# Combined convolution weights from 32-row groups in four row places, with a new order of the first steps

## The reference

```
p = hidden_states @ in_proj_w.T
h, gate = (p[..., :256], p[..., 256:])
conv = conv_general_dilated(h, conv_w, padding=[(3, 0)], feature_group_count=8) + conv_b
h = conv * silu(gate)
residual = h
hn = layernorm(h, ln_g, ln_b)
h = silu(hn @ fc_w.T + fc_b) @ cproj_w.T + cproj_b + residual
return h @ out_w.T
```

## Time and profile before

| | us |
|---|---|
| median of three runs | 369.46 (369.4 to 369.9) |
| the profiled execution's own time | 370.72 |
| its span, first to last instruction | 368.9 |
| TensorE busy | 323.3 (88%) |
| Vector busy | 261.1 (71%) |
| Scalar busy | 210.0 (57%) |
| GpSimd busy | 173.4 (47%) |

### The profile page before, as it was taken

The page is one execution under the profiler, slowest core; times in us unless marked ns, Lnnn a source line. Parts: engine busy times, 40 slices in busy tenths (PEclk is TensorE's granted clock), DMA queues, the critical chain, the costliest instruction groups (busy, mean ns, idle before and its releaser), DMA issues.

```text
span 368.9 us, 8839 instructions
## 1 busy us (share of the span) xinstructions
PE 323.3 (88%) x2692; PEld 295.2 (80%) x2692; DVE 261.1 (71%) x865; ACT 210.0 (57%) x430; POOL 173.4 (47%) x237
## 2 busy tenths in 40 slices
PE   3799999976777999999985989999798999999990
PEld 1789989866676999898975778888587999999990
DVE  3558988865873567769774699987796777677841
ACT  2354777635522355455438679898366668667330
POOL 1004677763464345886478677754211342244200
PEclk9999999987985999999999899999999999999997
DMA  8990011021132533421500300000000000000001
GB/s 274 431 367 1 16 37 40 29 61 29 43 97 59 186 85 92 140 60 53 165 23 29 115 2 2 3 3 0 3 3 0 2 16 16 14 14 0 16 14 32
DMA packets 17034, 23.73 MB, mean 64 GB/s; under 512 B 3424, under 2 KB 14176, under 8 KB 16208
## 3 DMA queue, kind: packets, MB, share of 16 engines
q1 hardware_dynamic: 13712, 17.97, 15.0%
q0 software_dynamic: 2272, 4.69, 3.9%
q10 hardware_dynamic: 1008, 0.53, 0.5%
HBM read 17.45 MB, written 6.73 MB: 66 GB/s over the span
## 4 chain that ended last, share of the span: by engine, by line
PE 44%; issue 12%; DVE 11%; POOL 9%; ACT 3%; POOLq 0%; DVEq 0%; ACTq 0%
PE ps L1985 8%; PE ps L1986 8%; PE ps L1817 6%; PE ps L1617 5%; POOL sb_w_lo L587 4%; PE ps L1619 4%; PE ps L1618 4%; PE ps L1806 3%; PE ps L2048 3%; POOL sb_xT_lo L580 1%; DVE sb_stage L1321 1%; DVE sb_x_in L1507 1%; POOL sb_rstd_hs L454 1%; PE ps L1782 1%; POOL answers L566 1%
## 5 line engine op out<-in xcount | busy, mean ns | idle before, releaser
L1985 PE MATMUL ps<-sb_w_hi,sb_fh_hi 128*128 128x256 f32 x256 | 61.2, 283 | 1.4 <-DVE sb_w_lo L925 0.7
L1986 PE MATMUL ps<-sb_w_lo,sb_fh_hi 128*128 128x256 f32 x256 | 59.8, 278 | 0.0
L1985 PEld LDWEIGHTS ps<-sb_w_hi,sb_fh_hi 128*128 128x128 f32 x256 | 48.2, 188 | 2.5 <-issue 1.1
L1986 PEld LDWEIGHTS ps<-sb_w_lo,sb_fh_hi 128*128 128x128 f32 x256 | 48.2, 188 | 0.0
L467 POOL DMA_INDIRECT routed<-sb_rows_of,sb_row x32 | 32.1, 1003 | 16.3 <-issue 10.1
L1617 PE MATMUL ps<-sb_w_hi,sb_rT_hi 128*128 x78 | 30.4, 390 | 7.3 <-issue 5.2
L1817 PE MATMUL ps<-sb_w,sb_stage 128*128 x234 | 34.9, 288 | 0.8 <-ACT sb_stage L752 0.8
L615 POOL TENSOR_TENSOR sb_w_lo<-sb_x_in,sb_w_hi 128x256 fp32r<-128x256 f32 x24 | 17.5, 757 | 35.4 <-DVE sb_w_hi L1553 35.4
L1817 PEld LDWEIGHTS ps<-sb_w,sb_stage 128*128 128x128 f32 x234 | 31.1, 202 | 1.2 <-issue 1.0
L566 POOL DMA_INDIRECT answers<-sb_stage x24 | 24.8, 1035 | 12.8 <-issue 8.2
L587 POOL TENSOR_TENSOR sb_w_lo<-sb_x_in,sb_w_hi 128x512 fp32r<-128x512 f32 x16 | 20.7, 1295 | 16.7 <-DVE sb_w_hi L1407 16.5
(11 more groups left out here) (308 smaller groups left out, 1031.0 us busy)
## 6 DMA issues: line engine op xcount, KB each, us to landing
sb_stage<-in_w SPq DMA_DIRECT2D x2, 1408.0 KB, 13.0
sb_stage<-routed SPq DMA_DIRECT2D x24, 65.0 KB
sb_w<-in_w SPq DMA_DIRECT2D x1, 1536.0 KB, 17.5
sb_x_in<-in_x_tok SPq DMA_DIRECT2D x1, 1024.0 KB, 8.7
sb_x_in<-in_ff_h SPq DMA_DIRECT2D x1, 1024.0 KB
sb_xT_in<-in_ff_h SPq DMA_DIRECT2D x1, 1024.0 KB
sb_got_first<-answers SPq DMA_DIRECT2D x4, 256.0 KB, 3.2
sb_w<-answers SPq DMA_DIRECT2D x4, 256.0 KB, 4.5
```

Source lines behind the costliest of these rows:

```text
L1985: mm(dst, w_hi, x_hi, start=start, stop=False)
L1986: last = mm(dst, w_hi, x_lo, start=False, stop=stop and exact)
```

## The change

`conv_own` holds, for each half, only the 32 by 32 blocks: 128 rows, two halves, 4 taps by 32 outputs, 128 KB. For each half TensorE makes four products of 32 rows and 128 columns; the group's rows select its place among the array's rows, and each of the eight products has a PSUM bank of its own. `front_of(t)` reads the four banks of a half in the order taps, groups, outputs. The first steps of the engines are put in another order:

```diff
@@ helpers
+        conv_own = conv_bd[:, :, 0:TAPS * GROUP_WIDTH]
+        def front_of(t):
+            return ps[:, t * GROUP_HEADS:(t + 1) * GROUP_HEADS, 0:TAPS * GROUP_WIDTH].rearrange("p g (k o) -> p k g o", o=GROUP_WIDTH)
@@ sync
-            for tile, src in ((w_h, "w_h"), (conv_bd, "conv_bd")):
+            for tile, src in ((w_h, "w_h"), (conv_own, "conv_own")):
                 sp.dma_start(tile[:, :, :], A[src]).then_inc(ld["front"], 16)
             sp.dma_start(xT_in[:, 0, :], A["xT"][:, 0, :]).then_inc(ld["x_first"], 16)
+            sp.dma_start(const[:, :], A["const"]).then_inc(ld["const"], 16)
+            sp.dma_start(conv_b[:, :], A["conv_b"]).then_inc(ld["bias"], 16)
@@ scalar
-            act.dma_start(const[:, :], A["const"]).then_inc(ld["const"], 16)
-            act.dma_start(conv_b[:, :], A["conv_b"]).then_inc(ld["bias"], 16)
-            for tile, src in ((ln_gb, "ln_gb"), (fc_b, "fc_b"),
-                              (cproj_b, "cproj_b"), (gate_wT, "gate_wT")):
+            for tile, src in ((ln_gb, "ln_gb"), (fc_b, "fc_b")):
                 act.dma_start(tile[:, :], A[src]).then_inc(ld["conv"], 16)
+            act.wait_ge(wt["memset"], MEMSETS)
+            nc.scalar.activation(touched[:, :], ones[:, 0:1], ACT.Silu)
...
-            for t in range(2):
+            def front_high(t):
                 act.wait_ge(wt["conv_mm"], t + 1)
-                nc.scalar.activation(front_hi[:, 0:TAPS, t * P:(t + 1) * P],
-                                     ps[:, t, :].rearrange("p (k o) -> p k o", o=P), ACT.Copy).then_inc(wt["front_hi"], 1)
+                nc.scalar.activation(front_hi[:, 0:TAPS, t * P:(t + 1) * P].rearrange("p k (g o) -> p k g o", o=GROUP_WIDTH),
+                                     front_of(t), ACT.Copy).then_inc(wt["front_hi"], 1)
...
             high_part(0)
+            for t in range(2):
+                front_high(t)
+            for tile, src in ((cproj_b, "cproj_b"), (gate_wT, "gate_wT")):
+                act.dma_start(tile[:, :], A[src]).then_inc(ld["conv"], 16)
             high_part(1)
-            act.wait_ge(wt["memset"], MEMSETS)
-            nc.scalar.activation(touched[:, :], ones[:, 0:1], ACT.Silu)
@@ tensor
             for t in range(2):
-                mm(ps[:, t, :], w_h[:, t, :], conv_bd[:, t, :], start=True, stop=True).then_inc(wt["conv_mm"], 1)
+                for g in range(P // GROUP_WIDTH):
+                    own = slice(g * GROUP_WIDTH, (g + 1) * GROUP_WIDTH)
+                    last = mm(ps[:, t * GROUP_HEADS + g, 0:TAPS * GROUP_WIDTH], w_h[own, t, :], conv_own[own, t, :], start=True, stop=True)
+                last.then_inc(wt["conv_mm"], 1)
...
-                    pe.wait_ge(wt["before"], 3)
+                    pe.wait_ge(wt["before"], 9)
```

More of the change, by code:

```diff
@@ L11 @@
 PAD = TAPS - 1
+GROUP_WIDTH = INNER // GROUPS
 EXPERTS, TOP_K, HIDDEN = 8, 2, 352
@@ L960, in _ @@
             V.memset(earlier[:, :, :], 0.0).then_inc(wt["before"], 1)
[L961 to L964, removed]
             V.memset(taken[:, :], 0.0).then_inc(wt["before"], 1)
@@ L969, in _, with low_part @@
             V.memset(upto_2[:, :], 0.0).then_inc(wt["before"], 1)
-            dve.wait_ge(wt["before"], 7)
+            dve.wait_ge(wt["before"], 6)
             V.memset(region_2[:, EXPERTS - 1:EXPERTS], -float((EXPERTS - 1) * REGION)).then_inc(wt["before"], 1)
+            def low_part(b):
+                dve.wait_ge(g0["x_hi"], b + 1)
+                wait(dve, g0["front"], b - 1)
+                V.tensor_tensor(xT_lo[:, b % 2, :], xT_in[:, b, :], xT_hi[:, b % 2, :].bitcast(fp32), ALU.subtract).then_inc(g0["x_lo"], 1)
+            dve.wait_ge(wt["front_hi"], 1)
+            V.tensor_tensor(front_lo[:, TAPS, :], w_gate[:, :], front_hi[:, TAPS, :].bitcast(fp32), ALU.subtract).then_inc(wt["front_lo"], 1)
+            low_part(0)
+            for t in range(2):
+                dve.wait_ge(wt["front_hi"], t + 2)
+                V.tensor_tensor(front_lo[:, 0:TAPS, t * P:(t + 1) * P].rearrange("p k (g o) -> p k g o", o=GROUP_WIDTH), front_of(t),
+                                front_hi[:, 0:TAPS, t * P:(t + 1) * P].bitcast(fp32).rearrange("p k (g o) -> p k g o", o=GROUP_WIDTH),
+                                ALU.subtract).then_inc(wt["front_lo"], 1)
+            dve.wait_ge(ld["const"], 16)
+            V.tensor_copy(before[:, :], const[:, C_BEFORE:C_BEFORE + P]).then_inc(wt["before"], 1)
+            V.tensor_scalar(base_row[:, :, :], const[:, C_BASE:C_BASE + EXPERTS].unsqueeze(1).to_broadcast([P, TILES, EXPERTS]),
+                            ident[:, 0:1], None, ALU.mult).then_inc(wt["before"], 1)
             V.tensor_copy(first_rows[:, :], const[:, C_ROW:C_ROW + max(PHASE_TILES)]).then_inc(wt["before"], 1)
@@ L998, in _ @@
             split3(conv_b3[:, :], whole_b, whole_b, b_part, b_rest, wt["conv_b3"])
-            dve.wait_ge(wt["front_hi"], 1)
-            V.tensor_tensor(front_lo[:, TAPS, :], w_gate[:, :], front_hi[:, TAPS, :].bitcast(fp32), ALU.subtract).then_inc(wt["front_lo"], 1)
-            for t in range(2):
-                dve.wait_ge(wt["front_hi"], t + 2)
-                V.tensor_tensor(front_lo[:, 0:TAPS, t * P:(t + 1) * P], ps[:, t, :].rearrange("p (k o) -> p k o", o=P),
-                                front_hi[:, 0:TAPS, t * P:(t + 1) * P].bitcast(fp32), ALU.subtract).then_inc(wt["front_lo"], 1)
             def small_weights():
@@ L1219, in _ @@
             h_flat = h[:, :, :].rearrange("p t f -> p (t f)")
-            def low_part(b):
-                dve.wait_ge(g0["x_hi"], b + 1)
-                wait(dve, g0["front"], b - 1)
-                V.tensor_tensor(xT_lo[:, b % 2, :], xT_in[:, b, :], xT_hi[:, b % 2, :].bitcast(fp32), ALU.subtract).then_inc(g0["x_lo"], 1)
-            low_part(0)
             dve.wait_ge(ld["conv"], 16 * 7)
@@ L2158, in layouts @@
     width = INNER // GROUPS
-    bd = np.zeros((2, P, TAPS, P), f)
-    for o in range(INNER):
-        t, g = o // P, o % P // width
-        bd[t, g * width:(g + 1) * width, :, o % P] = a["L0_attn_conv_w"][o]
-    A["conv_bd"] = np.ascontiguousarray(bd.reshape(2, P, TAPS * P).transpose(1, 0, 2))
+    by_group = a["L0_attn_conv_w"].reshape(2, P // width, width, width, TAPS)
+    A["conv_own"] = np.ascontiguousarray(by_group.transpose(1, 3, 0, 4, 2).reshape(P, 2, TAPS * width))
     A["conv_b"] = rows(a["L0_attn_conv_b"])
```

## The result

| | before | after |
|---|---|---|
| median, runs on one chip in turn | 369.43 (368.07 to 369.9, 4 runs) | 376.35 (375.35 to 378.4, 4 runs) |
| the profiled execution's own time | 370.72 | 376.35 |
| its span | 368.9 | 374.5 |

What follows compares the result with a forecast made beforehand. TensorE's back-to-back convolution batches were taken as the bound, handing on batch 0's shift. −0.3 us from `small_weights`' start and +0.9 from the clock made +0.6: span 368.9 to 369.5, median 370.1 us, range 368.2 to 372.3.

Steps and rivals of the forecast that it cites:

- The row places overlap: Combined weights on TensorE: 16 records overlap as column places do, taking 1.3 us and ending at 5.3.
- rival 1: Combined weights: row places don't overlap, products end at 7.8, loads land at 15.6 or later; 372.7 us; chance 15%.
- The gap on TensorE between front and `small_weights`: TensorE idles from 8.8 to 13.0 us, a gap of 3 to 5 us ended by `gate_wT`.
- rival 4: Small loads: their packets don't queue, so they land at 8.8 us; 365.4 us in all; chance 7%.
- the term of the two moved loads: `cproj_b` and `gate_wT`, issued later, land at 13.0 us; `small_weights` starts at 13.0 instead of 13.3, −0.3 us.
- The cross-check: Landing of `gate_wT`: its old 7.2 us copied onto an issue at 5.9 gives 13.1 us.
- The landing bounds of the range: Landing of the small loads: 11.0 us at the fast end (chance 20%), 15.6 or later at the slow end (15%).
- the clock: TensorE after the gap: rate rises 3.9 us after restart, at 16.9 against 16.27; the clock gives back 0.9 us.
- rival 2: TensorE after the gap: rate rises 5.5 us after restart, 370.9 us in all; later still, 371.5; chance 15%.
- the rest of `xT` to `w2` come about 1 us earlier: Large loads on the big queue land about 1 us earlier, and nobody waits for them once batch 0 is late.
- the handing on: Convolution batches on TensorE, 20.5 to 75 us, run back to back, so batch 0's shift is handed on nearly whole.

Runs made afterwards that it cites:

- e10: Changed kernel with the rest of `xT`, `x_tok` and `w13` laid out for packets of 1 to 2.8 KB instead of 7 to 11; 0.9984 of the kernel before.
- e4: Changed kernel with `cproj_b` and `gate_wT` joined in one tensor and one load at the same late place; 1.0112 of the kernel before.
- e6: Changed kernel with 26 products of 512 columns, results unread, ahead of the wait of `small_weights`; 1.0207 of the kernel before.
- e7: e1_early with `const` and `conv_b` back on Scalar's queue behind `w_gate`; 0.9923 of the kernel before.
- e1_early: Changed kernel with `cproj_b` and `gate_wT` issued early again, behind `fc_b`; 0.9999 of the kernel before.
- e8: e1_early with the 512 KB `conv_bd` and its two products of 512 columns, without row places; 0.9976 of the kernel before.
- e11: e7 with `const` and `conv_b` as the last issues on Scalar's queue, behind the table load; 0.9997 of the kernel before.
- e5: Changed kernel with `cproj_b` early and `gate_wT` late on its own semaphore, which only the gate's logits wait for; 0.9936 of the kernel before.
- e9: e1_early with the roundings of the experts' weights on Scalar, and Vector's low parts, one batch later; 0.9974 of the kernel before.

## Why the prediction was wrong

370.1 us were forecast, 368.2 to 372.3 as the range; it is 376.35.

**Right.** The row places overlap: 16 records in 1.24 us where 1.3 was taken from the column places, so rival 1 falls; the runs with them all show 1.24. The group starts at 4.40 (4.0 forecast), the front at 7.95 (6.95): the first piece of `xT` let Scalar start only at 5.63 (near 4.5 forecast), so Vector's low parts of the combined weights start at 6.56; both are hidden by the gap, as said. The gap on TensorE between front and `small_weights` is there and ended by `gate_wT`. The issues went out at 5.71 and 6.08 (5.4, 5.9). Small packets go one for one with large ones (52 beside 53, and again here), which speaks against rival 4. The Trainium skill, DMA: Bandwidth & Descriptors (Queues, rings and completion order), has an engine drain a whole packet of typically 9 to 17 descriptors before it turns to another ring; once both queues are in turn, this trace shows nothing of that at the grain of a microsecond.

**The step that failed: the term of the two moved loads.** The prediction took the first packet 1.1 us after the issue, 272 packets at 52 per us, and so 13.0 for the landing. Measured: first packet 3.2 us after the issue, 288 packets at 32 per us, 18.2 for the landing. Two errors of size. First: the earlier trace rows are from a moment when both queues were already in turn; the wait for a queue's first packet while the other keeps the engines full was not in them, and 1.1 us is what the first load of all takes on empty engines (issued at 0.74, first packets by 1.9). e10 shows that this part (3.2 to 3.9 us in six runs) does not depend on the packet size. Second, 52 per us came with packets of 7 KB on full engines; the later packets are larger (0.41 MB in 37 of them from 15 to 16 us, 21 small ones beside them), and even early the queues were not in step (50 to 23 from 9 to 10 us; why is open). e10 halves this part with short rows, e4 with half the packets. The cross-check, `gate_wT`'s old 7.2 us copied onto the new issue, shared the error: in the kernel before `gate_wT` was issued at 3.80, ahead of those packets. It agreed with the first estimate and so looked like support. The landing bounds of the range (11.0 to 15.6) held nothing that a load meets when it is issued *into* the large rows.

**A second term: the clock.** +0.9 us was taken for the slow rate, with the rise 3.9 us after the restart as before. It came 7.0 us after the restart and cost 2.4 us at the start, 1.5 more than the sum had. This is rival 2's mechanism, which put 0.8 us more on a rise after 5.5 us and 1.4 on one "later still". e6 shows that with work in the idle stretch this cost is gone. (Rivals 1 and 2 carry 30 of the hundredths, 28 of them slower; the text's 27 is a slip, and the sums of the chances use 28.)

**A third: "the rest of `xT` to `w2` come about 1 us earlier".** `x_tok` landed at 15.06 instead of 12.93. Fewer bytes ahead did not make up for two more issues on SP's queue (the rest of `xT` issued at 4.93 for 3.78). Of the 2.1 us about 1.2 are that later issue; the rest (9.6 us from issue to landing for 8.7) is within what the same order shows from one execution to the next. e7 against e1_early has the direction.

In sum −0.3 +0.9 were taken for the start, and it was +4.7 +2.4. What the forecast said of the handing on was right: 7.1 us at `gate_of(0)` are 7.1 at `gate_of(7)` and 5.6 in the span. It doesn't hold for every gain. e7's 2.7 us are handed on (2.8 at `gate_of(7)`), and so are e8's and e11's; of e1_early's 2.8 only 1.3 are and of e5's 3.5 only 0.5, since `gated(0)` waits behind `x_tok` there. e9 removes the wait for `w13` and not this one. Why its gain shrinks further, from 2.1 us at `gate_of(1)` to 0.7 at `gate_of(7)`, and what becomes of the gains behind the convolution stays open.

## What to carry to other kernels

A load that is tiny but has a row per partition costs by its packets. Issue it before the large rows, or expect 8 to 12 us beside rows of 7 to 11 KB; and do not put its issue behind an instruction that waits where somebody soon needs it. If a consumer waits for a count of loads, look whether it needs all of them: the load that landed last and held this kernel was one that the waiting products do not read. When the price of a load is read from a trace, note what ran at its issue; the same load at another moment is another price.

## What was not expected of the hardware

- A second queue's first packet came 3.2 to 3.9 us after its issue while another queue kept the 16 engines full, beside large rows or short ones. Beside large rows the two queues then went about one for one for some microseconds; beside short ones they did not (62 to 344).
- Four row places run float32 products of 32 rows at the same time: 16 records in 1.24 us, for 3.78 us of the same weights as two full products, in each of the ten kernels with them.
- The rate rose 3.9 us after the start of the front in the kernel before and 7.0 us after a gap of 8.0 us here, and the time did not follow the gap's length in other runs (6.6 us after 2.9); with products in the gap it was up when the small groups came.
- From 3 to 5 us, a single queue with loads of mostly 128 KB moved 206 and 179 GB/s (changed kernel), two queues with the same loads 298 and 307 (e7).
